# Gated unit of a two-layer block: the kernel values applied per token behind the output projection

## The reference

```python
u, v, base = silu(xn @ Wu.T + bu), silu(xn @ Wv.T + bv), silu(xn @ Wb.T + bb)   # 256, 256 and 128 wide
quad_q, quad_k = rope(base * qqw + qqb), rope(base * qkw + qkb)
quad_qk = jnp.einsum('bgne,bgme->bgnm', quad_q, quad_k)
kernel = jnp.square(jax.nn.relu(quad_qk / CHUNK + bias))       # CHUNK = 64, masked to n >= m
quadratic = jnp.einsum('bgnm,bgme->bgne', kernel, vch)
x = (u * (linear + quadratic)) @ Wo.T + bo
out = x + shortcut
```

## Time and profile before

| | us |
|---|---|
| median of 3 runs | 934.42 |
| lowest, highest | 934.37, 938.33 |
| the profiled execution's own time | 934.55 |
| its span (first to last instruction) | 932.8 |
| mean granted TensorE clock | 0.963 of full |
| TensorE, VectorE, ScalarE, GpSimd busy | 849.1, 638.1, 457.7, 548.5 |

### The profile page before, as it was taken

One profiled execution on the slowest core, in us unless ns is written; L12 is line 12 of the kernel. 1 busy time (PEld: TensorE's weight loads), 2 busy tenths in 40 slices (PEclk: granted clock), 3 DMA queues, 4 the chain that ended last, 5 costly groups with the idle time before them and its releaser, 6 DMA issues. The chain is left out here.

```text
span 932.8 us, 13290 instructions
## 1 busy us (share of the span) xinstructions
PE 849.1 (91%) x4792; PEld 442.0 (47%) x4792; DVE 638.1 (68%) x1060; ACT 457.7 (49%) x822; POOL 548.5 (59%) x319
## 2 busy tenths in 40 slices
PE   2797999999999999989799999999999937998598
PEld 2554444444444444544444444444444413784355
DVE  6887667777777775488677777777776354255853
ACT  2465455555555556555455555555555514435232
POOL 3323688688868878403476887788778821247400
PEclk9899999999999999999899999999999966999799
DMA  5000000000000000000000000000000002000001
GB/s 161 1 0 1 1 1 1 1 2 1 1 1 1 1 1 2 1 1 1 1 1 1 2 1 1 2 1 1 1 1 1 1 26 68 1 2 0 0 1 46
DMA packets 49595, 7.96 MB, mean 9 GB/s; under 512 B 42486, under 2 KB 47994, under 8 KB 49530
## 3 DMA queue, kind: packets, MB, share of 16 engines
q1 hardware_dynamic: 48666, 6.99, 4.7%
q10 hardware_dynamic: 864, 0.13, 0.1%
HBM read 5.92 MB, written 1.05 MB: 7 GB/s over the span
## 5 line engine op out<-in xcount | busy, mean ns | idle before, releaser
L977 DVE TENSOR_REDUCE part<-psum 128x2 f32<-128x1024 f32 x256 | 313.3, 1224 | 137.5 <-PE psum L511 137.5
L399 POOL TENSOR_TENSOR space<-space 128x1024 f32<-128x1024 f32 x160 | 380.6, 2379 | 38.3 <-ACT space L752 20.5
L752 ACT ACTIVATE space<-psum 128x512 f32<-128x512 f32 x512 | 264.5, 602 | 156.4 <-PE psum L531 155.5
L546 PE MATMUL psum<-space,vb 128*64 128x512 f32 x1024 | 247.7, 605 | 0.0
L511 PE MATMUL psum<-kh,qh 64*128 64x512 f32 x512 | 128.5, 498 | 13.8 <-DVE part L977 13.4
L404 POOL TENSOR_TENSOR space<-space 128x1024 f32<-128x1024 f32 x30 | 71.6, 2385 | 106.2 <-DVE space L991 106.2
L511 PEld LDWEIGHTS psum<-kh,qh 64*128 64x128 f32 x512 | 48.2, 185 | 154.4 <-DVE part L977 120.3
L546 PEld LDWEIGHTS psum<-space,vb 128*64 128x64 f32 x1024 | 62.4, 136 | 106.5 <-issue 101.1
L531 PE MATMUL psum<-qh,kh 64*128 64x512 f32 x512 | 103.5, 401 | 0.0
L531 PE MATMUL psum<-ql,kh 64*128 64x512 f32 x512 | 102.4, 396 | 0.0
L531 PE MATMUL psum<-qh,kl 64*128 64x512 f32 x512 | 101.9, 394 | 0.0
(11 more groups left out here) (164 smaller groups left out, 887.6 us busy)
## 6 DMA issues: line engine op xcount, KB each, us to landing
ql<-nmx SPq DMA_DIRECT2D x256, 0.5 KB, 2.0
w1s<-in_L_ffn_W SPq DMA_DIRECT2D x4, 256.0 KB, 2.7
w2s<-in_L_ffn_W SPq DMA_DIRECT2D x4, 256.0 KB
out<-x SPq DMA_DIRECT2D x4, 256.0 KB, 2.1
x<-in_L_attn_x SPq DMA_DIRECT2D x2, 256.0 KB, 4.4
wproj<-in_L_attn_Wq SPq DMA_DIRECT2D x1, 512.0 KB, 6.7
x<-in_L_attn_x SPq DMA_DIRECT2D x1, 512.0 KB, 7.6
wout<-in_L_attn_Wout SPq DMA_DIRECT2D x1, 512.0 KB, 6.7
```

The lines of the kernel that those rows point to most:

```text
L399: pool.tensor_tensor(to, pt[0] if u == 1 else to, pt[u], ALU.add)\
L546: last = pe.matmul(outp[rows(h), :], vb[:, place(m)[1], kt, :], pt[kt][:, h, :], start=(kt == 0), stop=(kt == TILES - 1))
L752: act.activation(pt[kt][:, h, :], key_scores[kt % 2][h], ACT.Exp).then_inc(exp_made, 1)
L977: dve.tensor_reduce(to[:, half, :], scores.rearrange("p (h k) -> p h k", h=2), AX_X, ALU.max, negate=True)\
```

## The change

- The gate products v * u are projected with Wo as they are (three projections a half, `gau_out(h, n)`), and the kernel values scale the projected rows, one number per token and partition (`take_gau`), with the shortcut as the added term; token 1 takes two such steps.
- The sum over the partitions becomes a matmul whose stationary operand is a 128 x 128 tile of the product and whose moving operand is one column of ones: twelve one-column results a half, tokens on the partitions, in one bank. VectorE makes the kernel values of them in two small instructions (`gau_kernel`). `relus`, `gau_mix` and `mix` go.
- The heads go from VectorE to ScalarE, the gate products all to VectorE (two of them inside `after_ffn` of the last chunk).
- The 8 column root is split in two of 4, the one for the rows first.
- The four lists are reordered: the last `gau_in` goes ahead of the position product, both halves' projections stand before the turns of the last part, and `final(1)` behind the gates of the last chunk. The first four projections use the wide banks.

```diff
-        kern = mine("kern", [P, 3, CW])
-        vu = mine("vu", [P, 3, 2, CW])
-        mix = mine("mix", [P, BATCH, 2, CW])
+        kern = mine("kern", [P, BATCH, 2, 3, T])
+        vu = mine("vu", [P, BATCH, 3, 2, CW])
...
+        def gau_at(h, n):
+            m = 3 * h + n
+            return wide(FIRST_OUT + m) if m < 4 else by_token(m)
         def other(m):
             return psum[:, (6 + m % 2) * CW:(7 + m % 2) * CW]
         FIRST_IN = CHUNKS * UP
-        FIRST_PAIR = FIRST_IN + CHUNKS * IN
+        FIRST_OUT = FIRST_IN + CHUNKS * IN
...
+            elif m < FIRST_OUT:
+                pe.wait_ge(silu_made, m - FIRST_IN + 1)
             elif m < FIRST_PAIR:
-                pe.wait_ge(silu_made, m - FIRST_IN + 1)
+                pe.wait_ge(gau_taken, m - FIRST_OUT + 1)
...
+                 + [("turned_q", 0), ("dots", 0), ("turned_q", 1), ("dots", 1)]
+                 + [("rows", n) for n in range(8, 12)])
...
+            def root(k, which=0, first=True):
+                wanted[0] += first
                 roots[0] += 1
-                pool.wait_ge(var_made, roots[0])
-                flat = inv[:, k, 0:2 if both else 1, :].rearrange("p s t -> p (s t)")
-                pool.tensor_tensor(flat, flat, half_power[:, 0:2 * T if both else T], ALU.pow).then_inc(inv_made, 1)
+                pool.wait_ge(var_made, wanted[0])
+                pool.tensor_tensor(inv[:, k, which, :], inv[:, k, which, :], half_power[:, 0:T], ALU.pow).then_inc(inv_made, 1)
...
-            def products(h):
...
-                root(2 * CHUNKS + ch, both=True)
+                root(2 * CHUNKS + ch, 1)
+                root(2 * CHUNKS + ch, 0, False)
                 shortcut(ch)
-            products(0)
-            products(1)
...
             def gau_dots(h):
-                for n in (0, 2, 1):
-                    pe.wait_ge(prod_made, 3 * h + {0: 1, 2: 2, 1: 3}[n])
-                    pe.matmul(next_other(), c["ones_square"][:, :], prod[:, n, :], start=True, stop=True).then_inc(dots_made, 1)
-            def gau_out(h):
-                for l in range(BATCH):
-                    wait_by_token(pe, CHUNKS + 2 * h + l)
-                    pe.wait_ge(mix_made, h + 1)
+                at = next_other()
+                for i, n in enumerate((0, 2, 1)):
+                    pe.wait_ge(prod_made, 3 * h + i + 1)
                     for t in range(T):
-                        for e in range(2):
-                            last = pe.matmul(by_token(CHUNKS + 2 * h + l)[:, t * P:(t + 1) * P], mix[:, l, e, t * P:(t + 1) * P],
-                                             wt[:, (W_O + e) * P:(W_O + e + 1) * P], start=(e == 0), stop=(e == 1))
-                    last.then_inc(gau_made, 1)
+                        last = pe.matmul(at[:, n * T + t:n * T + t + 1], prod[:, n, t * P:(t + 1) * P], ones[:, 0:1], start=True, stop=True)
+                last.then_inc(dots_made, 1)
+            def gau_out(h, n):
+                m = 3 * h + n
+                if m < 4:
+                    wait_wide(pe, FIRST_OUT + m)
+                else:
+                    pe.wait_ge(token_out, m - 1)
+                pe.wait_ge(vu_made[h], n + 1)
+                for t in range(T):
+                    for e in range(2):
+                        last = pe.matmul(gau_at(h, n)[:, t * P:(t + 1) * P], vu[:, h, n, e, t * P:(t + 1) * P],
+                                         wt[:, (W_O + e) * P:(W_O + e + 1) * P], start=(e == 0), stop=(e == 1))
+                last.then_inc(gau_made, 1)
...
             turn(CHUNKS + 3, 3)
+            gau_in(3, 3)
             turn_position(0)
+            gau_out(0, 0)
             gau_dots(0)
-            gau_in(3, 3)
-            gau_out(0)
+            gau_out(0, 1)
+            gau_out(0, 2)
             turn_position(1)
+            gau_out(1, 0)
+            gau_dots(1)
+            gau_out(1, 1)
+            gau_out(1, 2)
             turn(2 * CHUNKS, PAIRED[0])
-            gau_dots(1)
             turn(2 * CHUNKS + 1, PAIRED[1])
             gate_up(0)
-            gau_out(1)
             gate_up(1)
...
-            def relus(h):
...
+            def gau_heads(h):
+                act.wait_ge(silu_made, (3 + h) * IN)
+                if h:
+                    act.wait_ge(prod_made, 3)
+                for l, n in ((1, 0), (0, 1), (0, 0), (1, 1)):
+                    last = act.activation(heads[:, l, n, :], uvb[:, 2 * l + h, IN - 1, :], ACT.Identity, bias=c["qk_cols"][:, 2 + n:3 + n],
+                                          scale=c["qk_cols"][:, n:n + 1])
+                last.then_inc(heads_made, 1)
...
             keep(CHUNKS + 3, 3, c["lng"][:, 0:1], c["lnb"][:, 0:1])
-            relus(0)
+            gau_heads(0)
             silu(3, 3)
+            gau_heads(1)
             keep(2 * CHUNKS, PAIRED[0])
-            relus(1)
             keep(2 * CHUNKS + 1, PAIRED[1])
...
-            def after_ffn(ch):
+            def after_ffn(ch, first=lambda: None, second=lambda: None):
...
-                dve.wait_ge(inv_made, 2 * ch + CHUNKS + 1)
+                first()
...
-                dve.wait_ge(inv_made, 2 * ch + CHUNKS + 2)
+                second()
...
-            def gau_heads(h):
-                dve.wait_ge(silu_made, (3 + h) * IN)
+            def gau_same(h):
+                dve.wait_ge(heads_made, h + 1)
                 if h:
-                    dve.wait_ge(dots_made, 3)
-                for l, n in ((1, 0), (0, 1), (0, 0), (1, 1)):
-                    last = dve.tensor_scalar(heads[:, l, n, :], uvb[:, 2 * l + h, IN - 1, :], c["qk_cols"][:, n:n + 1],
-                                             c["qk_cols"][:, 2 + n:3 + n], ALU.mult, ALU.add)
-                last.then_inc(heads_made, 1)
-            def gau_same(h):
-                dve.wait_ge(heads_made, h + 1)
+                    dve.wait_ge(dots_made, 1)
                 dve.tensor_tensor(prod[:, 0, :], heads[:, 0, 0, :], heads[:, 0, 1, :], ALU.mult).then_inc(prod_made, 1)
                 dve.tensor_tensor(prod[:, 2, :], heads[:, 1, 0, :], heads[:, 1, 1, :], ALU.mult).then_inc(prod_made, 1)
             def gau_cross(h):
                 dve.wait_ge(turned_q, h + 1)
-                dve.tensor_tensor(prod[:, 1, :], other(OTHER.index(("turned_q", 4 * h))), heads[:, 0, 1, :], ALU.mult).then_inc(prod_made, 1)
-                link(dve.tensor_tensor(vu[:, 0, :, :], uvb[:, h, 2:4, :], uvb[:, h, 0:2, :], ALU.mult))
-            def gau_mix(h, between=lambda k: None):
+                dve.tensor_tensor(prod[:, 1, :], other(OTHER.index(("turned_q", h))), heads[:, 0, 1, :], ALU.mult).then_inc(prod_made, 1)
+            def products(h, n):
+                l, m = ((0, 0), (1, 0), (1, 1))[n]
+                dve.wait_ge(silu_made, (2 * l + h + 1) * IN)
+                dve.tensor_tensor(vu[:, h, n, :, :], uvb[:, 2 * m + h, 2:4, :], uvb[:, 2 * l + h, 0:2, :], ALU.mult).then_inc(vu_made[h], 1)
+            def gau_kernel(h):
+                dve.wait_ge(dots_made, h + 1)
+                dots = other(OTHER.index(("dots", h)))[:, 0:3 * T].rearrange("p (n t) -> p n t", t=T)
+                link(dve.scalar_tensor_tensor(out=kern[:, h, 0, :, :], in0=dots, scalar=1.0 / CHUNK, in1=over_last(c["rel"][:, :], T),
+                                              op0=ALU.mult, op1=ALU.add))
+                dve.scalar_tensor_tensor(out=kern[:, h, 1, :, :], in0=kern[:, h, 0, :, :], scalar=0.0, in1=kern[:, h, 0, :, :],
+                                         op0=ALU.max, op1=ALU.mult).then_inc(kern_made, 1)
+            def take_gau(h, n, to, other_term):
+                m = 3 * h + n
+                dve.wait_ge(gau_made, m + 1)
                 dve.wait_ge(kern_made, h + 1)
-                dve.wait_ge(vu_made, h + 1)
-                if h:
-                    dve.wait_ge(gau_made, 2)
-                dve.tensor_tensor(mix[:, 0, :, :], vu[:, 0, :, :], over_mid(kern[:, 0, :], 2), ALU.mult)
-                between(0)
-                dve.tensor_tensor(vu[:, 1, :, :], vu[:, 1, :, :], over_mid(kern[:, 1, :], 2), ALU.mult)
-                between(1)
-                link(dve.tensor_tensor(vu[:, 2, :, :], vu[:, 2, :, :], over_mid(kern[:, 2, :], 2), ALU.mult))
-                dve.tensor_tensor(mix[:, 1, :, :], vu[:, 1, :, :], vu[:, 2, :, :], ALU.add).then_inc(mix_made, 1)
-                between(2)
+                for t in range(T):
+                    last = dve.scalar_tensor_tensor(out=to[:, t, :], in0=gau_at(h, n)[:, t * P:(t + 1) * P], scalar=kern[:, h, 1, n, t:t + 1],
+                                                    in1=other_term[:, t, :], op0=ALU.mult, op1=ALU.add)
+                last.then_inc(gau_taken, 1)
             def add_gau(n):
                 ch = PAIRED[n]
-                dve.wait_ge(gau_made, n + 1)
+                l, h = batch_half(ch)
                 dve.wait_ge(short_made, ch + 1)
-                dve.tensor_tensor(xc(ch), by_token(n).rearrange("p (t d) -> p t d", d=DIM), xb[:, ch, :, :], ALU.add).then_inc(token_out, 1)
```

(79 more changed lines are left out.)

12 lines of the change are left out of this document (7 added, 5 removed).

## The result

The changed kernel took 920.26 us (median of 4 runs, 916.83 to 922.55) against 934.39 before: ratio 0.9831, interval 0.9802 to 0.986. Six more runs later gave 918.12 (915.36 to 922.43), ratio 0.9821, interval 0.9791 to 0.985. The forecast was 919.0.

What follows compares the result with a forecast made beforehand. TensorE was busy 91%, but a relay of waits between engines bound the edited last 100 us. 932.8 - 17.0 + 1.75 = 917.55, with one clock loss of 1.5: 919.0; 8-in-10 range 915.5 to 925.5.

Steps and rivals of the forecast that it cites:

- The relay: Tail up to the third gate/up group at 911.16: waits passing between engines; that group starts 17.0 us earlier.
- The heads: VectorE in the tail: heads leave it, 2.07 us in the first half and 5.99 in the second.
- The walk: Tail followed engine by engine in the times of before; third gate/up group at 894.2 and not 911.16.
- The sums at 0.107 to 0.11 a record: Sums over partitions on TensorE: 24 one-column records at 0.11, 2.65 us a half, ends 1.5 and 4.1.
- The clock: Projections behind the one-column sums: one stretch at half rate, 1.5 us, on the chain behind the first, mostly covered behind the second.
- signs of being wrong: One-column stretch of 4 us or more, takes 2, products 1.8 on the chain, or clock 0.50 over 4 us between 862 and 890.
- VectorE as the chain of the second half: From 869.25 VectorE's 9.45 us to 878.7 set the time; TensorE's 8.2 us lie beside it, ending at 877.3.
- The gate products in `after_ffn`, costed at nothing: Before the last turn: two products fill VectorE's waits, last rows ready at 852.2; without cover each costs 1.2 to 1.8.
- The takes: VectorE: four scale-and-add instructions reading each projection, 1.15 us, with bounds 1.13 and twice that.
- The VectorE rival: VectorE becomes the bound by more if reading PSUM doubles its scale-and-adds: 6.9 us, time 925.5; chance 0.11.
- the slow one: Rival on both sums: one-column matmuls bound by latency, 0.74 us a record, time 949; chance 0.04.
- no change: Rival: gain doesn't reach the end, as something that doesn't move sets gate/up groups or last chunks; about 933; chance 0.04.

Runs made afterwards that it cites:

- The doubled sums: Changed kernel with each one-column matmul of the sums issued twice: median 931.31 us, ratio 0.9946 to before.
- the 128-column variant: Changed kernel with the sums over partitions moving 128 columns of ones in place of one: median 917.99 us, ratio 0.9819 to before.
- the core alone: Changed kernel with heads back on VectorE, four of six gate products back on GpSimd and one 8-column root: 927.20 us, ratio 0.9924 to before.
- the filled order: Changed kernel with the first projection moved ahead of the last gau_in and two gate products put behind after_ffn: 920.45 us, ratio 0.9828 to before.
- one root: Changed kernel with the single 8-column root as before in place of two: 919.92 us, ratio 0.9854 to before.

## Why the prediction was right

- **The relay goes, and is worth about 15 us.** Right: 14.5 in the tail, forecast 15.5; 42.65 us from the turn to the third group, forecast 42.4. (Among the signs I had also put that group 16 to 17 us earlier; from the turn it is 15.2.) About half is the core, that projections no longer wait for kernel values: 8.7 us by the tail, about 7 by the ratio. Taking the products off GpSimd brings 3.9 of the rest, and by a path that I had only for the heads: its long operations stretch whatever VectorE does beside them.
- **The heads.** I listed them as removed from the chain at 5.99 us. Where they stood they were worth 2.6 us, and putting them back on VectorE in the changed kernel costs nothing. The walk didn't count removed terms one by one, and that is why the sum held: it followed each engine to its next wait.
- **The sums at 0.107 to 0.11 a record.** Right, 2.57 us a half at full clock. The doubled sums show it again. The Trainium skill's rule for the load (TensorE: Matmul & The Clock Gate, section LDWEIGHTS: stationary columns over 1.2 GHz) agrees: 128 over 1.2 GHz is 0.107 us. So does the 128-column variant, whose 24 records take 2.69 us on the chain and not 2.57.
- **The clock.** One fall was taken, at 1.5 us. One fell in the profile, but behind the second sums, where I had called it "mostly covered". It lasted for the whole of two projections, cost TensorE 3.3 us, and 1.8 of them came through, which the 128-column sums measure. The step that failed is "behind the second it is mostly covered", and that 1.5 stood near 1.8 is luck: the right size for the wrong place. One of my own signs of being wrong came true with it, a granted clock of 0.50 for more than 4 us between 862 and 890 (from 876 to past 882). Nor is one fall the rule. In the seven profiles with 24 one-column records a half it fell behind 7 of the 14 stretches, from none in the core alone to both in the filled order.
- **VectorE as the chain of the second half.** Right only where the clock holds: TensorE then waits 1.27 and 0.22 us (I had 0.35 for the second). With the fall TensorE is the chain all the way.
- **The gate products in `after_ffn`, costed at nothing.** Wrong by 0.3 us of waiting. I had the last rows a microsecond before their turn, and the turn waited 0.31 for them. The product was 1.66 and the roots beside it 2.00 and 1.92: I had stretched VectorE's operation and left GpSimd's as it was. The Trainium skill (SBUF — State Buffer, section Who interferes with whom) says that a VectorE operation with two SBUF inputs and a GpSimd one that reads SBUF exclude each other; the second to come waits. The trace agrees: both roots start beside a product (849.46 and 854.23 are its ends) and end 0.87 us behind it, nearly the 1.06 that a root takes alone.
- **The takes.** Right: 1.13 with an operand in PSUM. The VectorE rival is out. So is the slow one, and so is no change.

## What to carry to other kernels

Price a removed operation by what its engine waits for next: the longest link of the chain of before, 5.99 us, was worth 2.6 where it stood, and moving it to another engine cost as much elsewhere. A rewrite that lets TensorE run ahead of a small scalar result was worth 7 to 9 us. When GpSimd and VectorE work side by side, stretch both in the sum. And when matmuls become narrow to save nothing, keep their moving operand wide if the load bounds them anyway: here 128 columns cost 0.1 us a half more than one, and the clock of what followed stayed up in all three profiles. The medians don't show that gain by itself (917.99 against 918.12).

## What the runs showed of the hardware

- Behind 24 records (2.6 to 2.9 us) that move one column, with TensorE never idle in them, the granted clock fell to 0.50 in 7 of 14 cases: behind the second sums in the changed kernel (both profiles), with VectorE's heads and with one root, behind both in the filled order, behind the first with products on GpSimd, and behind neither in the core alone (3.82 us for the projections behind both). Behind the same records moving 128 columns it was 1.00 in all 6 cases, in the three profiles with them. With 48 one-column records it fell twice, before they had ended. What decides between one case and the next is not settled.
- An idle stretch doesn't always bring the fall. Behind 2.23 us ahead of the second half's projections it fell in the kernel before (5.44 us for 32 records) and not in that kernel with its products on VectorE (3.81). After 2.45 us ahead of the position product it fell in both: in the kernel before as the product started (2.08 us for its two records), in the other 0.8 us after the start, so that they took 1.29.
- A tiny VectorE instruction (128 x 12) took 3.51 us beside a GpSimd product and ended within 0.03 us of it, and four of 512 columns took 7.67; elsewhere they are 0.17 and 2.07.
- A float32 matmul record with 128 stationary columns took 0.107 us with 1 moving column and 0.112 with 128. Sixteen records that move 128 columns took 1.95 us with 128 stationary columns and 1.04 with 64.
